# The first layer's ternary matrices made beside the experts' tiles, and one stage for what follows them

## What is computed

```python
x = x + tanh(g_xattn[0]) * _L0_xattn_ref(_layernorm(x), itok, ctx_2048, ctx_2048, ctx_2048)
x = x + tanh(g_ffn[0]) * _L0_ffn_ref(_layernorm(x), L0_ffn_W_up, L0_ffn_W_gate, L0_ffn_W_down)
...
def _L0_xattn_ref(...):     # four experts; the token's id says which; the context serves as all weights
    y = (silu(x @ Wg[e].T) * (x @ Wu[e].T)) @ Wd[e].T
...
def ternary_quant(w):
    scale = mean(abs(w)) + 1e-8
    q = clip(round(w / scale), -1, 1) * scale
def _L0_ffn_ref(...):
    hidden = silu(x @ wu.T) * (x @ wg.T)
    return hidden @ wd.T
```

## Time and profile before

| | us |
|---|---|
| median of 3 runs (3543.55 to 3548.8) | 3547.64 |
| the profiled execution | 3543.03 |
| its span in the trace | 3541.3 |
| experts, first instruction to the last y (43.8 to 191.9) | 148 |
| gather back and add (first gather 194.14, last add ends 219.27) | 25 |
| ternary_matrices (first load 220.74, last copy ends 286.75) | 66 |
| scaled_gate and transposed_parts (287.59 to 326.05) | 38 |
| first matmul of ternary_ffn | at 327.32 |

### The profile page before, as it was taken

One profiled execution on the slowest core, in us unless ns is written; L12 is line 12 of the kernel. 1 busy time (PEld: TensorE's weight loads), 2 busy tenths in 40 slices (PEclk: granted clock), 3 DMA queues, 4 the chain that ended last, 5 costly groups with the idle time before them and its releaser, 6 DMA issues. The chain is left out here.

```text
span 3541.3 us, 63656 instructions
## 1 busy us (share of the span) xinstructions
PE 2737.0 (77%) x21394; PEld 1415.9 (40%) x21394; DVE 2572.9 (73%) x4720; ACT 1835.0 (52%) x2658; POOL 701.9 (20%) x577
## 2 busy tenths in 40 slices
PE   5925999785799999999986677786797547758983
PEld 3413444333365656565653333333111223224541
DVE  5555667566799999999984666524797787986547
ACT  2334433232499999999982433313676022434551
POOL 4422000012110101010104233203012503550012
PEclk8966999896899999999998788897998769978996
DMA  4251431200000000000001100100431000023301
GB/s 171 73 202 48 143 119 48 92 0 15 18 13 7 13 7 13 7 13 13 1 12 51 36 0 0 60 15 12 96 72 45 28 20 1 0 65 64 64 7 51
DMA packets 65283, 151.89 MB, mean 43 GB/s; under 512 B 11792, under 2 KB 20000, under 8 KB 63328
## 3 DMA queue, kind: packets, MB, share of 16 engines
q1 hardware_dynamic: 62320, 140.43, 13.1%
q0 software_dynamic: 2800, 9.18, 0.9%
HBM read 93.61 MB, written 24.38 MB: 33 GB/s over the span
## 5 line engine op out<-in xcount | busy, mean ns | idle before, releaser
L1507 DVE TENSOR_REDUCE s_top<-ps 128x1 f32<-128x512 f32 x1024 | 657.8, 685 | 32.8 <-PE ps L1402 32.3
L1476 ACT ACTIVATE s_prob<-ps,s_shift,m_sq 128x1024 int16<-128x1024 f32 x512 | 615.1, 1202 | 31.2 <-DVE s_shift L1515 31.2
L1402 PE MATMUL ps<-s_ks,s_qs 128*128 128x512 f16 x1024 | 352.4, 386 | 61.4 <-issue 15.3
L1407 PEld LDWEIGHTS ps<-ident,s_prob 128*128 128x128 f16 x4096 | 273.2, 98 | 123.3 <-DVE m_o L1525 52.1
L1407 PE MATMUL ps<-ident,s_prob 128*128 128x128 f16 x4096 | 314.6, 220 | 0.7 <-ACT s_prob L1476 0.5
L1395 PE MATMUL ps<-s_ks,s_qs 128*128 128x512 f16 x1024 | 307.2, 382 | 1.1 <-ACT s_prob L1476 0.5
L1482 ACT ACTIVATE s_probT<-ps 128x1024 f16<-128x1024 int16 x256 | 262.1, 1024 | 6.6 <-PE ps L1407 6.4
L246 PE MATMUL ps<-ident,s_parts 128*128 128x128 f16 x768 | 90.9, 291 | 165.9 <-POOL s_parts L237 164.2
L1520 DVE CAST s_probT<-ps 128x1024 f16<-128x1024 int16 x256 | 174.6, 682 | 3.0 <-PE ps L1407 2.9
L2166 DVE TENSOR_SCALAR s_prob<-ps,s_cap 128x1024 f32<-128x1024 f32 x128 | 158.2, 1271 | 25.2 <-PE ps L2075 25.2
L2747 DVE TENSOR_REDUCE s_ntop<-ps 128x1 f32<-128x512 f32 (+3 forms) x256 | 107.5, 484 | 86.6 <-PE ps L2607 86.6
(11 more groups left out here) (379 smaller groups left out, 5990.6 us busy)
## 6 DMA issues: line engine op xcount, KB each, us to landing
s_qs<-m_qT SPq DMA_DIRECT2D x144, 128.0 KB, 2.5
s_ks<-m_kT SPq DMA_DIRECT2D x96, 128.0 KB, 2.4
numbers<-s_numbers SPq DMA_DIRECT2D x21, 512.0 KB, 2.8
s_slabs<-numbers SPq DMA_DIRECT2D x21, 512.0 KB, 3.8
m_ks<-context_parts SPq DMA_DIRECT2D x12, 512.0 KB, 7.5
expert_rows<-s_y SPq DMA_DIRECT2D x19, 256.0 KB, 2.0
s_rows_in<-in_ctx SPq DMA_DIRECT2D x16, 256.0 KB, 3.0
x_sb<-in_x SPq DMA_DIRECT2D x1, 4096.0 KB, 14.2
```

The lines of the kernel that those rows point to most:

```text
L1402: pe.matmul(quarter_at(q), qs[:, hb, bass.ds(t * P, P)], ks[:, hb, cols(q, 512)], start=True, stop=True).then_inc(s.top_scored, 1)
L1407: j = pe.transpose(turned(half, F16)[:, cols(m, P)], prob[:, u, cols(8 * half + m, P)].bitcast(F16), k.ident[:])
L1476: act.activation(prob[:, u, cols(half, HALF)], pair(half).rearrange("p m n -> p (m n)"), ACT.Exp, bias=shift[:, u:u + 1], scale=sq[:, bass ...
L1507: dve.tensor_reduce(top4[:, u, q:q + 1], quarter_at(q), AX.X, ALU.max).then_inc(s.top_read, 1)
```

## The change

- `layer0_xattn` and `layer0_ffn` become one function `layer0`. The first two weight matrices' place serves as cT, and x's own place and hT serve as buffers for slabs while the experts run (`nat`, six slabs; `whole`, two).
- **experts** gets the ternary work up to the clip. SP loads slabs 0 to 5 in iterations 0 to 2 and slab i-1 in iterations 7 to 12, and stores cT in iteration 13. x is not loaded here. DVE sums slab i-2 (`absolute`, iterations 2 to 13), clips slab i-7 (`clip`, iterations 7 to 18), and finishes a matrix in iterations 5, 9 and 13 (`step_size`), in which it waits for POOL's sum over partitions. POOL makes that sum after the gather of the same iteration. ACT multiplies slab i-6 (`multiply`, iterations 6 to 17) and takes `copy_hidden` over from DVE.
- A new stage **expert_rows_added** holds the rest: x is loaded in four parts, POOL gathers the tiles of y back and takes one root for each tile, DVE adds, takes the statistics, the offset and the low half and copies the turned tile, ACT normalises, takes the high half and copies the weights' banks (24, spread over 17 turns), PE turns both.
- `ternary_matrices`, `scaled_gate` and the first use of `transposed_parts` are gone.

```diff
-def experts(k, cT, rows, rows_loaded, tokens, places, weights_of):
+def experts(k, cT, rows, rows_loaded, tokens, weights_of, matrices, scales, numbers, spare):
...
+            u = g % NATS
+            return k.x[:, cols(u, 4), :].rearrange("p t d -> p (t d)") if u < 4 else more_nats[:, u - 4, :]
...
-            sp.dma_start(k.x[:], k.x_in.rearrange("(t p) d -> p t d", p=P)).then_inc(s.x_loaded, 16)
-            sp.dma_start(k.context_parts, cT[:].rearrange("p l c n -> p (l c n)")).then_inc(s.context_stored, 16)
-            for a in range(A):
-                sp.wait_ge(s.y_ready, a + 1)
-                sp.dma_start(k.expert_rows[cols(a, P), :], y[:, a % YR, :]).then_inc(stored[a % YR], 16)
...
+            for i in range(A + 2):
+                if 1 <= i < A:
+                    sp.wait_ge(s.up_ready, i)
+                if i < NATS // 2:
+                    load(2 * i)
+                    load(2 * i + 1)
+                if NATS <= i - 1 < LAST:
+                    sp.wait_ge(s.scaled, i - NATS)
+                    load(i - 1)
+                if i == LAST + 1:
+                    sp.dma_start(k.context_parts, cT.rearrange("p l c n -> p (l c n)")).then_inc(s.context_stored, 16)
+                if i >= 2:
+                    sp.wait_ge(s.y_ready, i - 1)
+                    sp.dma_start(k.expert_rows[cols(i - 2, P), :], y[:, (i - 2) % YR, :]).then_inc(stored[(i - 2) % YR], 16)
             sp.wait_ge(s.context_stored, 16)
+            for u in range(YR):
+                sp.wait_ge(stored[u], 16 * len(range(u, A, YR)))
...
+                if i % SLABS == 1 and 0 <= i // SLABS - 1 < M:
+                    m = i // SLABS - 1
+                    pool.wait_ge(s.sum_ready, m + 1)
+                    pool.partition_all_reduce(total[:, m:m + 1], sums[:, m:m + 1], P, RADD).then_inc(s.total_ready, 1)
...
+            def multiply(g):
+                m = g // SLABS
+                act.wait_ge(s.inv_ready, m + 1)
+                if g >= 2:
+                    act.wait_ge(s.numbers_ready, g - 1)
+                act.activation(whole[:, g % 2, :], nat(g), ACT.Copy, scale=inv[:, m:m + 1]).then_inc(s.scaled, 1)
+            def copy_hidden(a):
+                act.wait_ge(s.hid_turned, a + 1)
+                if a >= 2:
+                    act.wait_ge(s.down_ready, a - 1)
+                act.activation(hidT[:, a % 2, :, :, :], k.ps16[:, HIDDEN, :].rearrange("p (l c n) -> p l c n", l=2, c=DC),
+                               ACT.Copy).then_inc(s.hid_copied, 1)
...
+                if 0 <= i - 6 < LAST:
+                    multiply(i - 6)
...
+                if 0 <= i - 1 < A:
+                    copy_hidden(i - 1)
...
+            def absolute(g):
+                dve.wait_ge(nat_loaded[g % NATS], 16 * (g // NATS + 1))
+                v.later(dve.tensor_reduce(part[:, cols(g % SLABS, SLAB // GROUP)],
+                                          nat(g).rearrange("p (g n) -> p g n", n=GROUP), AX.X, ALU.add,
+                                          apply_absolute_value=True))
+            def step_size(m):
+                scale = scales[:, m:m + 1]
+                v.catch_up()
+                v.done(dve.tensor_reduce(part2[:], part[:].rearrange("p (g n) -> p g n", g=SLAB // GROUP), AX.X, ALU.add))
+                dve.tensor_reduce(sums[:, m:m + 1], part2[:], AX.X, ALU.add).then_inc(s.sum_ready, 1)
+                dve.wait_ge(s.total_ready, m + 1)
+                v.done(dve.tensor_scalar(scale, total[:, m:m + 1], 1.0 / float(F * D), 1e-8, ALU.mult, ALU.add))
+                dve.reciprocal(inv[:, m:m + 1], scale).then_inc(s.inv_ready, 1)
+            def clip(g):
+                dve.wait_ge(s.scaled, g + 1)
+                dve.tensor_scalar(numbers[:, g, :], whole[:, g % 2, :], 1.0, -1.0, ALU.min, ALU.max
+                                  ).then_inc(s.numbers_ready, 1)
...
-                if 0 <= i - 1:
-                    copy_hidden(i - 1)
-            dve.wait_ge(s.x_loaded, 16)
+                if 0 <= i - 7 < LAST:
+                    clip(i - 7)
+                if 0 <= i - 2 < LAST:
+                    absolute(i - 2)
+                if i % SLABS == 1 and 0 <= i // SLABS - 1 < M:
+                    step_size(i // SLABS - 1)
...
+def expert_rows_added(k, places, hT, matrices, numbers, factor, scale):
...
+        def bank_range(t):
+            return range(len(banks) * t // (T + 1), len(banks) * (t + 1) // (T + 1))
...
+            for q in range(4):
+                sp.dma_start(k.x[:, cols(q, 4), :], rows_of[:, cols(q, 4), :]).then_inc(x_loaded[q], 16)
...
+            for t in range(GR):
+                gather(t)
+            pool.memset(power[:], -0.5).then_inc(s.power_ready, 1)
+            pool.wait_ge(s.power_ready, 1)
             for t in range(T):
+                pool.wait_ge(s.var_ready, t + 1)
+                pool.tensor_tensor(k.rstd[:, t:t + 1], var[:, t:t + 1], power[:], ALU.pow).then_inc(s.rstd_ready, 1)
+                if t + GR < T:
+                    pool.wait_ge(s.added, t + 1)
+                    gather(t + GR)
...
+            def add(t):
                 x = k.x[:, t, :]
+                if t % 4 == 0:
+                    dve.wait_ge(x_loaded[t // 4], 16)
                 dve.wait_ge(got[t % GR], 16 * (t // GR + 1))
                 dve.tensor_tensor(x, x, got_y[:, t % GR, :], ALU.add).then_inc(s.added, 1)
...
+            def offset_of(t):
+                dve.wait_ge(s.rstd_ready, t + 1)
+                dve.tensor_scalar(offset[:, t:t + 1], k.mv[:, t, 0:1], k.rstd[:, t:t + 1], -1.0, ALU.mult, ALU.mult
+                                  ).then_inc(s.offset_ready, 1)
...
+            dve.tensor_tensor(factor, k.gate[:, 4:5], scale, ALU.mult)
+            for t in range(T + 4):
+                if t < T:
+                    add(t)
+                if 0 <= t - 3 < T:
+                    low(t - 3)
+                if t < T:
+                    dve.wait_ge(s.added, t + 1)
+                    dve.bn_stats(bn[:, t, :], k.x[:, t, :]).then_inc(s.stats_ready, 1)
+                if 0 <= t - 4:
+                    copy(t - 4)
+                if 0 <= t - 1 < T:
+                    offset_of(t - 1)
+                if t < T:
+                    dve.wait_ge(s.stats_ready, t + 1)
+                    dve.bn_aggr(k.mv[:, t, :], bn[:, t, :]).then_inc(s.mv_ready, 1)
+                    dve.wait_ge(s.mv_ready, t + 1)
+                    dve.tensor_scalar(var[:, t:t + 1], k.mv[:, t, 1:2], LN_EPS, None, ALU.add).then_inc(s.var_ready, 1)
...
+            turn_weights_of(0)
+            for t in range(T):
+                turn_weights_of(t + 1)
+                pe.wait_ge(s.parts_ready, t + 1)
+                if t >= R:
+                    pe.wait_ge(s.copied, t - R + 1)
+                for m in range(2 * DC):
+                    i = pe.transpose(k.ps16[:, t % R, cols(m, P)], parts[:, t % R, m // DC, cols(m % DC, P)], k.ident[:])
+                i.then_inc(s.turned, 1)
...
+            copy_weights_of(0)
+            for t in range(T):
+                copy_weights_of(t + 1)
+                act.wait_ge(s.offset_ready, t + 1)
+                if t >= R:
+                    act.wait_ge(s.parts_ready, t - R + 1)
+                act.activation(normal[:, t % R, :], k.x[:, t, :], ACT.Identity, bias=offset[:, t:t + 1],
+                               scale=k.rstd[:, t:t + 1]).then_inc(s.normal_ready, 1)
+                if t >= R:
+                    act.wait_ge(s.turned, t - R + 1)
+                act.wait_ge(s.normal_ready, t + 1)
+                act.activation(parts[:, t % R, 0, :], normal[:, t % R, :], ACT.Copy).then_inc(s.hi_ready, 1)
...
-        run = [layer0_xattn, layer0_ffn, layer1_xattn, layer1_ffn, layer2_xattn, layer2_ffn, layer3_xattn, layer3_ffn]
+        run = [layer0, layer1_xattn, layer1_ffn, layer2_xattn, layer2_ffn, layer3_xattn, layer3_ffn]
...
-            nats = [sb2("nat%d" % m, [P, F * D // P], F32) for m in range(2)]
-            ternary_matrices(k, matrices, k.scale, 0.0, 1e-8, nats)
-        scaled_gate(k, factor[:], 4, k.scale[:, 2:3])
-        hT = sb("hT", [P, 2, DC, N], F16)
-        transposed_parts(k, hT)
...
+                experts(k, cT, rows, rows_loaded, tokens, weights_of,
+                        (k.i.L0_ffn_W_up, k.i.L0_ffn_W_gate, k.i.L0_ffn_W_down), k.scale, numbers, hT)
+            expert_rows_added(k, places, hT, w, numbers, factor[:], k.scale[:, 2:3])
```

More of the change, by code:

```diff
@@ L793, in _, with turn_weights_of @@
         @s.block.tensor
         def _(pe):
[L795 to L803 removed]
+            def turn_weights_of(t):
+                for n in bank_range(t):
+                    _, _, slab, h = banks[n]
+                    if n >= 4:
+                        pe.wait_ge(s.weights_copied, n - 3)
+                    for b in range(8):
+                        i = pe.transpose(k.ps16[:, 4 + n % 4, cols(b, P)], slab[:, cols(8 * h + b, P)], k.ident[:])
+                    i.then_inc(s.weights_turned, 1)
@@ L805, in _ @@
+            turn_weights_of(0)
```

(33 more changed lines are left out.)

201 lines of the change are left out of this document (71 added, 130 removed).

## The result

The changed kernel takes 3556.44 us (median of 7 runs, 3548.34 to 3560.89) against 3547.64 for the one before: the ratio is 1.0028, with a 95% interval of 1.0016 to 1.0040. It is slower by 9 us, where 3521 was forecast. Its profiled execution took 3560.89 us, with a span of 3559.1.

A forecast was written before the change was run, and what follows sets the result against it. Bound: in the experts stage, a ring of POOL's queue and one gather, 6.83 us a tile. Last-stage gain 71.8 less experts growth 45.1 gives 26.7 us, from median 3547.6 to 3521; range 3497 to 3543 for 8 in 10.

The forecast's parts named there:

- The ring and DVE's row: Experts stage: POOL's queue and one gather set 6.83 us a tile; DVE's work with clip and slab sum, 6.69, just fits.
- The changes of set: Experts iterations 5, 9, 13: POOL changes operation set for the sum over partitions and back, 7.1 us each way, 34.3 together.
- Rival 1: Experts stage: only POOL's change back costs, the change toward the sum is free; kernel 3500 us, chance 0.12.
- rival 4: Experts stage: POOL's six changes of set take longer beside transfers, gain gone from 11.6 us each; 3562 at 14; chance 0.08.
- The clip: Experts stage: POOL operations wait for DVE's clip, +1.1 us a ring, 4.4 in rings 7, 8, 11 and 12.
- rival 5: Experts stage: the sum of a slab on DVE holds up POOL, +26 us; kernel 3547, no change; chance 0.05.
- The slabs: Experts stage: slab loads delay gathers, +1 us for all together, bounds 0 to 3.75 in each of four plain rings.
- The store: Experts iteration 13: the 4 MB context store meets the gathers of iterations 12 and 13, +1 us, at most 7.5.
- Start and tail: Experts stage: less traffic before the first gather, 0, perhaps -3 us; after the last gather PE and ACT cost +4.4.
- The last stage: New stage after the experts: DVE bounds at 3.03 us a tile, ACT and PE hidden; 61.4 us replacing 133.2.
- Rival 2: Experts stage: gathers meet slabs and the context's store, 3.75 us each, 20 us more loss; kernel 3541, chance 0.09.
- Rival 3: New last stage: DVE and POOL get in each other's way, 3.8 us a tile, +11; kernel 3532, chance 0.08.

The follow-up runs named there:

- e10_early_all: Changed kernel with ACT's tile work before weight copies, sum on PE, slabs gated, context store in four parts, gathers two iterations earlier: 3461.10 us, ratio 0.9772.
- e7_clip_after: Changed kernel with DVE taking a slab's absolute sum before the clip of another slab, not after: 3559.83 us, one run.
- e5_store16: Changed kernel with the 4 MB context store issued in iteration 16 of the experts stage instead of iteration 13: 3542.61 us, one run.
- e4_sum_pe: Changed kernel with the sum over partitions done as a matmul with ones on PE instead of on POOL: 3537.18 us, ratio 0.9986.

## Why the prediction was wrong, step by step

- **The ring and DVE's row**: right. Three of four plain rings stayed at 6.8 us beside the sums of slabs (one took 7.99), and from the fifth tile on DVE waits for gathered rows at the end of every ring but the three that a sum over partitions stands in. DVE's row is 6.59 in e10_early_all, for 6.69.
- **The changes of set** (34.3 us): 32.2 us. Rival 1, a free change toward the sum, falls with 6.18, 6.08 and 5.89 us; rival 4, changes of 11.6 us or more beside slabs, with 7.25 to 7.76. The Trainium skill's figure (GPSIMD Engine Reference, 2.1 Instruction dispatch: about 6 us for the first call after loading) fits the direction toward the sum, and is 1.3 to 1.8 us short of the way back. The row of 7.11 also lay 1.1 above it, not within a microsecond.
- **The clip** (+1.1 a ring): +0.6 from statistics to gather. **The sum of a slab** (0): right, by e7_clip_after; rival 5 falls. **The slabs** (+1): about 2 us, nearly all in the ring of 9.41.
- **The store** (+1, at most 7.5): +8.2 in its ring, 7.5 by e5_store16. The value was taken at the wrong end of its bounds: of the two gathers that the store meets, the one that no change of set hides paid for all of it.
- **Start and tail**: the fifth statistics came 1.7 us sooner (0, perhaps -3), the stretch from the last statistics to the last y grew by 2.4 us (4.4). The store came out 7 us too low; the sums, the clip, the start and the tail were each about 2 us too high. That 44.6 agrees with 45.1 is luck.
- **The last stage** (61.4 us): 104.0 us, and this is where the forecast failed. The step that failed is the overlap: the sentence that ACT's 45 us and PE's transposes are hidden beside DVE's 58. Busy times were compared engine by engine, and each was indeed below DVE's. But a queue holds what stands behind a wait, and the order PE: tile, weights; ACT: weights, tile makes one chain of six links out of work that has no such dependence: 0.75 + 0.83 + 1.10 + 0.92 + 0.89 + 0.67 = 5.16 by the starts from 287.26 to 292.42. With one line moved the stage took 64.8 us from the last y. So DVE's row was right in kind (2.80 instead of 3.03, and 3.27 where ACT's two banks bind), and 3.4 us are left, of which 2.0 are the way from the last y to the first transfer, 3.5 us and not 1.5, with the last store of y in it. The largest pace gives 61.4 + 14 x 0.8 = 72.6 us, not 74, and neither end of that range allows for one queue waiting for another.
- **Rival 2** (gathers meet the slabs) was there but mostly covered: one ring shows it in the changed kernel (9.41), and several in e4_sum_pe, as soon as POOL's stalls are gone. **Rival 3** had the right place and a wrong mechanism: 3.8 us a tile from DVE against POOL, where 5.15 to 6.06 came from the queues.

In sum: from the last y on, the kernel before took 135.4 us and the changed one 104.0, a gain of 31.4 where 71.8 was forecast; with 44.6 lost ahead of it, layer 0 ends 13.2 us later. The 71.8 was itself 2.2 us too low, since it sets 61.4 us counted from the last y against 133.2 counted from the first gather back. With ACT's line moved layer 0 ends 27.0 us sooner than before, close to the 26.7 that was forecast, but only since the stage's 3.4 us too many are made up by these 2.2 and by 1.4 us less in the experts.

## What to carry to other kernels

When two streams of work share in-order queues, write down for every engine what it does in one turn and follow who waits for whom around the turn; only then compare busy times. Where a chain closes over a neighbouring tile, it was enough here to move one operation past the other on one engine. A load whose buffer is free should be asked for as soon as it is free: two iterations of cover made a slow gather, a bulk store and slabs beside it all harmless, and it also paid in the kernel before.

## What the runs showed of the hardware

- A sum over partitions between elementwise operations on POOL kept its queue from other work for 13.3 to 13.9 us in the changed kernel, both directions together, and for 12.7 to 15.5 us in the six experiments that have it (5.9 to 7.9 toward the sum, 6.7 to 7.7 back), beside other transfers. A matmul with ones on PE gives the sum without it.
- DVE's clip (int32 to f16, 128x2048, 1.22 us) lengthens whatever POOL has beside it: root 0.94 to 1.68, low half 1.15 to 1.74, the issue of a gather 1.00 to 1.72. The sum of absolute values (2.28 us) lengthens nothing. The Trainium skill (SBUF — State Buffer, Who interferes with whom) says both: DVE's two-port modes lock the pair of ports that it shares with GpSimd, and a `tensor_reduce` never contends. The rows agree: the root ended 0.04 us after the clip, and the gather's issue in e7_clip_after 0.1 us after it (124.97 and 124.86). The lengthening, 0.6 to 0.7 us, is below the clip's 1.22, since the two overlap only in part.
- A gather of 256 KB took 3.4 us from issue to use in the plain ring of the earlier trace rows, 3.3 to 6.3 in rings with a slab of 1 MB (in e4_sum_pe the two longest, 5.7 and 6.3, had the slab issued within 0.8 us of the gather, and one with the slab 3.5 us ahead took 3.6), and about 11 with a store of 4 MB issued 1.4 us before it (172.61 to 183.67).
